# Self-attention slots of a decoder layer: output projection moved ahead of the transposes, attention times V moved behind the scores

## The reference

```
x = x + self_attention(layernorm(x))        # fixed point, 16 heads of 64
x = x + cross_attention(layernorm(x), ctx)  # 16 heads of 64
x = x + experts(layernorm(x))               # two experts of width 1024, with rank-16 updates

def make_fxp(t):   # 12 fraction bits, clipped to +-(8 - 1/4096)
    return trunc(clip(t, -c, c) * 4096) / 4096
# self-attention:
q, k, v = make_fxp(x @ Wqkv) split into heads
dots = make_fxp(q @ k.T / 8)
attn = make_fxp(softmax(dots))
out  = make_fxp(attn @ v)
out  = make_fxp(out @ Wproj + bias)
```

## Time and profile before

| | |
|---|---|
| median of the runs | 730.09 us |
| span of the profiled execution | 730.2 us |
| PE busy | 672.8 us, 92% |
| DVE busy | 550.0 us, 75% |
| ACT busy | 413.7 us, 57% |
| POOL busy | 272.6 us, 37% |
| mean granted TensorE clock | 0.995 of full |

### The profile page before, as it was taken

One profiled execution on the slowest core, in us unless ns is written; L12 is line 12 of the kernel. 1 busy time (PEld: TensorE's weight loads), 2 busy tenths in 40 slices (PEclk: granted clock), 3 DMA queues, 4 the chain that ended last, 5 costly groups with the idle time before them and its releaser, 6 DMA issues.

```text
span 730.2 us, 15676 instructions
## 1 busy us (share of the span) xinstructions
PE 672.8 (92%) x5186; PEld 551.7 (76%) x5186; DVE 550.0 (75%) x1142; ACT 413.7 (57%) x1443; POOL 272.6 (37%) x610
## 2 busy tenths in 40 slices
PE   5998879989998899878989999999999889999997
PEld 4777768777886788766777877787788777888986
DVE  5879887887888789757767776677667668787775
ACT  4677756767776777764455455445544563433432
POOL 1166754454445534535354344234333532010110
PEclk9999999999999999999999999999999999999999
DMA  9135100000000000050000000000000000000000
GB/s 312 49 111 150 60 30 1 1 1 1 0 0 0 0 0 0 0 153 1 1 2 16 1 1 1 14 0 0 0 0 0 0 1 1 2 30 0 29 29 29
DMA packets 17002, 18.75 MB, mean 26 GB/s; under 512 B 2851, under 2 KB 15427, under 8 KB 16963
## 3 DMA queue, kind: packets, MB, share of 16 engines
q1 hardware_dynamic: 15330, 15.11, 6.4%
q0 software_dynamic: 1632, 3.15, 1.5%
HBM read 16.16 MB, written 2.10 MB: 25 GB/s over the span
## 4 chain that ended last, share of the span: by engine, by line
PE 35%; POOL 7%; DVE 6%; ACT 3%; issue 3%; DVEq 0%; POOLq 0%; ACTq 0%
PE bank L405 9%; PE bank L407 8%; PE bank L406 8%; POOL p_f L363 6%; PE bank L583 3%; ACT e_sb L889 2%; PE bank L595 2%; PE bank L607 1%; DVE mx L1164 1%; PE bank L729 1%; PE bank L741 1%; DVE bn_st L966 1%; DVE oT_lo L1206 1%; POOL p_int L316 0%; DVE v_sb L1137 0%
## 5 line engine op out<-in xcount | busy, mean ns | idle before, releaser
L363 POOL TENSOR_SCALAR p_f<-e_sb,rsum 128x128 f32<-128x128 f32 x256 | 95.6, 398 | 156.7 <-DVE rsum L1199 156.7
L316 POOL TENSOR_SCALAR p_int<-e_sb,rsc 128x128 int16<-128x128 f32 x256 | 116.2, 475 | 6.3 <-issue 5.7
L889 ACT ACTIVATE e_sb<-bank,neg_max 128x128 f32<-128x128 f32 x256 | 90.1, 380 | 12.1 <-DVE neg_max L1168 11.9
L804 ACT ACTIVATE sgn<-bank 128x512 bf16<-128x512 f32 x96 | 57.2, 598 | 57.6 <-PE bank L407 57.6
L819 ACT ACTIVATE e_sb<-si 128x128 f32<-128x128 int16 x256 | 75.1, 303 | 0.0
L1021 DVE SCALAR_TENSOR_TENSOR ri<-sgn,bank 128x512 int16<-128x512 bf16 x96 | 62.5, 677 | 7.3 <-ACT sgn L804 6.5
L875 ACT COPY q_sb<-bank 128x512 f32<-128x512 f32 x32 | 18.8, 587 | 84.5 <-PE bank L407 84.5
L311 POOL TENSOR_TENSOR rsc<-rsum,growth 128x8 f32<-128x8 f32 x32 | 6.7, 209 | 156.0 <-DVE rsum L1047 156.0
L889 ACT ACTIVATION_READ_ACCUMULATOR e_sb<-bank,neg_max 128x1 f32 x256 | 55.9, 218 | 0.0
L405 PE MATMUL bank<-xnT_hi,wqkvT_lo 128*128 128x512 f32 x128 | 53.6, 419 | 2.2 <-DVE ri L1021 1.3
L1175 DVE COPY aT_sb<-bank 128x512 f32<-128x512 f32 x64 | 41.2, 685 | 12.7 <-PE bank L583 12.5
(11 more groups left out here) (162 smaller groups left out, 2039.5 us busy)
## 6 DMA issues: line engine op xcount, KB each, us to landing
x_sb<-in_x SPq DMA_DIRECT2D x4, 512.0 KB, 10.3
wqkv_raw<-in_L_attn_w_qkv SPq DMA_DIRECT2D x2, 1024.0 KB, 10.2
out<-x_sb SPq DMA_DIRECT2D x8, 256.0 KB, 2.2
wqkv_raw<-in_L_attn_w_qkv SPq DMA_DIRECT2D x2, 512.0 KB, 5.1
wp_raw<-in_L_attn_w_proj SPq DMA_DIRECT2D x1, 1024.0 KB, 12.3
raw_b<-in_L_xattn_Wq SPq DMA_DIRECT2D x2, 512.0 KB, 3.3
wq_hi<-in_L_xattn_Wq POOLq DMA_DIRECT2D x2, 512.0 KB, 4.1
wo_hi<-in_L_xattn_Wo POOLq DMA_DIRECT2D x2, 512.0 KB, 8.4
```

Of the source, the lines that this page charges most:

```text
L316: i = nc.gpsimd.tensor_scalar(p_int[:, t, :], e_sb[:, t, :], rsc[:, t:t + 1], -0.5, ALU.mult, ALU.add)
L363: i = nc.gpsimd.tensor_scalar(p_f[:, t, :], e_sb[:, t, :], rsum[:, t:t + 1], 0.0, ALU.mult, ALU.add)
L804: nc.scalar.activation(sgn[:, m % 2, :], proj_ps[m % 2][:, :], ACT.Sign).then_inc(a_sgn, 1)
L889: last = nc.scalar.activation(e_sb[:, t, :], s_ps[hh][:, (t % 4) * P:(t % 4 + 1) * P], ACT.Exp, bias=neg_max[:, t:t + 1], scale=DH ** -0.5 ...
```

## The change

On PE, project_out(n-3) moves ahead of a_transpose(n-2), and a_attend(n-2) moves from ahead of the V blocks to the slot's end, behind a_scores. On ACT, a_out_sign(n-2), which reads a_attend's result, moves behind the signs of the scores. On DVE, a_out(n-2) moves from right behind the reciprocal to the slot's end, behind the clips. No operation, size or semaphore is added or removed.

```diff
@@ -512,23 +512,23 @@
                 if first:
                     wait(pe, w_lo, (10, 0, 12, len(PREP), 0, 0, 0, 0)[s])
                 lag2 = not (first and s < 2)
+                if not (first and s < 3):
+                    project_out(n - 3, (s - 3) % NP, a_olo, a_pj, (wpT_hi, wpT_lo), (a_z, 2 * g))
                 if lag2:
                     a_transpose(n - 2)
-                if not (first and s < 3):
-                    project_out(n - 3, (s - 3) % NP, a_olo, a_pj, (wpT_hi, wpT_lo), (a_z, 2 * g))
                 if s == NP - 1:
 
                     normed_T(g + 1, lambda: wait(pe, a_ri, BLOCKS * (g + 1)))
-                if lag2:
-                    p = (s - 2) % NP
-                    gg = g if s >= 2 else g - 1
-
-                    a_attend(n - 2, p, BLOCKS * gg + (block_index(1) + 4 if p < 4 else block_index(3) + 4))
                 if s < 4:
                     for i in range(2):
                         j = 2 * s + i
                         a_block(g, base + 2 + i, (j % 4, 2 * E + 512 * (j // 4)), False)
                 a_scores(n, s, BLOCKS * g + base + 2)
+                if lag2:
+                    p = (s - 2) % NP
+                    gg = g if s >= 2 else g - 1
+
+                    a_attend(n - 2, p, BLOCKS * gg + (block_index(1) + 4 if p < 4 else block_index(3) + 4))
 
             normed_T(0, lambda: wait(pe, w_lo, 4))
             a_weights_T(PREP_PARTS[1])
@@ -840,8 +840,6 @@
                     if s == NP - 1:
                         xnT_high(g + 1)
                     a_exp(n - 1, 1)
-                if lag2:
-                    a_out_sign(n - 2)
                 if s < 4:
                     sign_of(g, base + 2)
                     sign_of(g, base + 3)
@@ -849,6 +847,8 @@
                     wait(act, a_S, 2 * n + i + 1)
                     wait(act, a_si, 2 * n + i - 1)
                     nc.scalar.activation(s_sgn[:, i, :], s_ps[i][:, :], ACT.Sign).then_inc(a_ssgn, 1)
+                if lag2:
+                    a_out_sign(n - 2)
 
             xnT_high(0)
             a_weights_high(PREP_PARTS[1])
@@ -1100,8 +1100,6 @@
                     xnT_low(g + 1)
                 if not (first and s == 0):
                     a_recip(n - 1)
-                if not (first and s < 2):
-                    a_out(n - 2)
                 if s < 4:
                     if s == 0 and not first:
                         wait(dve, a_av, NP * g - 4)
@@ -1118,6 +1116,8 @@
                 for i in range(2):
                     wait(dve, a_si, 2 * n + i + 1)
                     V.tensor_scalar(si[:, i, :], si[:, i, :], LOW, None, ALU.max).then_inc(a_clip, 1)
+                if not (first and s < 2):
+                    a_out(n - 2)
 
             xnT_low(0)
             a_weights_low(PREP_PARTS[1])
```

## The result

The changed kernel takes 783.8 us (median of 4 runs, 781.7 to 785.8) against 730.05 us: a ratio of 1.0735, interval 1.0715 to 1.0755, slower. The forecast was 782 us, 770 to 798. The profiled execution took 783.5 us and spans 781.7 from its first instruction to its last; the same 1.8 us lie between time and span in every run whose span is on record.

The account below looks back on a forecast made before the run. The prediction took an 8.35 us loop through aT, exponentials and p_int to bound short slots and PE's own work long ones; 730.2 + 45.4 (chain) + 6.5 (clock) = 782 us, range 770 to 798.

Parts of the forecast that it names:

- The loop of 8.35 us: Self-attention: transposes, aT copy, exponentials, reciprocal, p_int and next transposes form a loop that sets the slot time before the change.
- short slots: Slots 4 to 6 of a group of eight, without V blocks; predicted to go from 8.35 to 9.8 us, +1.45.
- The rival in which the projection fills the gap: The projection runs in PE's idle time if oT_lo comes by T+6.6 in short slots: 730 us, at best 707; chance 0.04.
- The rival with short slots alone: Only short slots stall, since V fixes run during the exponentials and long slots stay at 10.05: about 752 us; chance 0.08.
- The terms of the chain: Added slot times in self-attention because late a_out delays the projection and the transposes behind it: together +45.4 us.
- Long slots: Slots 0 to 3, which carry V blocks; predicted to go from 10.05 to 11.7 us, +1.65.
- With y_out: In slot 2 of a later group, y_out's two DVE operations stand in front of si too: +2.85 us.
- POOL's wo_lo beside V's fixes at the start of group 1: POOL's wo_lo stretches DVE's V fixes, 2.32 instead of 0.78 us; this 1.5 us now lies on the chain.
- The clock: Long PE gaps in self-attention lower TensorE's clock: falls at half of 15 gaps, 0.9 us each, +6.5, bounds 0 and 22.
- the rival of a fall at nearly every gap: The clock falls at nearly every gap, or in long slots too: about 797 us; chance 0.15.
- Group 0: First group of self-attention, measured from slot 2: predicted 63.65 us against 55.31, +8.3.
- POOL in the way of a_out in group 0: POOL's low parts block a_out, oT_hi meeting each of five 2.4 us operations: 794 us; chance 0.05.

Follow-up runs that it names:

- The swap of two calls on PE: The changed kernel with a_transpose(n-2) put back ahead of project_out(n-3), late a_out and late attend kept: 736.5 us, 1.0096 against the kernel before.
- y_out early: The changed kernel with transposes ahead of projection, exponentials ahead of the aT copy, y_out ahead of the reciprocal: 734.2 us, 1.0061 against the kernel before.
- the best kernel: The y_out early kernel with aT's copy between the exponentials' halves in groups 1 to 3, group 0 in the old order: 727.9 us, 0.9967.

## Why the prediction was right

*The loop of 8.35 us binds short slots; PE's idle 1.2 us is its slack.* Right. Filling the gap gave nothing (projection alone: 8.35 still), and taking aT out of the loop's way gave 8.0 and 7.6.

*The projection waits for a_out and holds the transposes.* Right: 30 waits, 56.1 us. The swap of two calls on PE gives 47 us back. The rival in which the projection fills the gap failed where it was said to: oT_lo came at T+8.1, not T+6.6. The rival with short slots alone failed as well, PE waits 1.4 to 1.5 us in long ones.

*The terms of the chain.* Short slots 9.70 for 9.8. Long slots 11.45 for 11.7: DVE's run of eight was 3.48 by starts where I had 3.57 by ends, a_out 1.86 (212.37 to 214.23) for 1.98, and the projection 1.54 for 1.60. The two blocks of PE take 3.03 us (225.44 to 228.47 in the earlier trace rows), not the 2.8 that I wrote, so PE's wait in short slots is 2.35 and not 2.6; that changes no slot, since PE waits either way. With y_out 12.65 for 12.9, slot 7 10.7 for 10.75 (both in the kernel with the K block twice, where no fall disturbs them). POOL's wo_lo beside V's fixes at the start of group 1 was on the chain as foreseen, but stretched them by 0.6 us only, not 1.5 (1.1 in the kernel with the K block twice). In the changed kernel, DVE:

```profile
107.64 1.37 DVE L1025 TENSOR_SCALAR v_sb<-ri 128x512 f32<-128x512 int16 x2
```

The span without falls, as the kernel with the K block twice has it, is 771.5 us: 730.2 + 41.3, where I had 45.4.

*The clock.* The term that was mis-sized the other way: 781.7 - 771.5 = 10.2 us, I had 6.5, well inside its bounds of 0 and 22. I had 15 long gaps, half of them with a fall at 0.9 us. There were 12 of 1.87 to 2.63 us in groups 1 to 3 and ten were followed by a fall, about 1 us each. So by number the rival of a fall at nearly every gap was the nearer one, and what held the sum down was the price. For that price the prediction's own bound was worked out too low: 2.03 us scaled by 1.98/1.09 are 1.66 us more and not 1.5, 25 us for 15 gaps and not 22. The transposes at 1.2 GHz, which no row of before showed (changed kernel, PE):

```profile
262.76 1.08 PE L464 MATMUL bank<-ident_b,p_int 128*128 128x128 bf16 x8
```

The full transposes took 1.08 us for 0.62, the projection before them 2.34 (260.42 to 262.76) for 1.54. The two errors, 4.1 too many in the chain and 3.7 too few in the clock, all but cancel, which is luck; the total is better than its parts. The base was off a little as well: a span of 730.2 belongs to an execution of an estimated 732 us, by the 1.8 us between time and span, so 782 was a forecast of the span, 781.7, rather than of the median, 783.8.

*Group 0.* 63.1 us for 63.65. No fall there, although three gaps of 2.6 were counted: its 2.4 us of idle time came in two pieces, since the scores waited 1.05 to 1.19 us for K while POOL's low parts held up the Q fix, and only 1.2 to 1.4 us were left before the projection. I had named that collision for oT_hi and not for Q; it cost no time, slots stayed at 9.70.

*POOL in the way of a_out in group 0* did not come in the changed kernel: no oT_hi or oT_lo there took over 0.75 us. It came where the order moved a_out against POOL (2.73 us for oT_lo with the transposes first, 2.49 for oT_hi with y_out early). The Trainium skill (SBUF — State Buffer, "Who interferes with whom") says that DVE in a two-port mode and GpSimd exclude each other for a whole instruction. The 2.49 us fit this, since oT_hi ends just behind wq_lo; in which mode it ran no row tells.

What stays open: the best kernel loses 1.2 us at the hand-over to cross-attention, 22.7 us from the transposes of the last slot 7 to the second ones after it, against 21.5 before. Whether another order there would keep them was not tried.

## What to carry to other kernels

An idle gap in front of a wait may be the slack of a loop through other engines: follow that loop once around, and compare its length with each engine's own work, before moving work into the gap. In an in-order queue whatever stands ahead of the head of such a loop lends it all its own waits, so a producer moved late and its consumer moved early can cost together what neither costs alone (by the ratios +54 us here, +7 and +19 apart, and the 19 are a wait for aT that the whole change does not have). Before an order is changed, look at what the moved instructions will run beside: here DVE's 0.5 to 0.7 us operations took over 2 us beside POOL's. When stalls lie between matmuls, count their effect on the clock too, and time a kernel with harmless work in the gap to see its price.

## What was not expected of the hardware

Doing the K block twice made the kernel 9.7 us faster, with the granted clock at 2.4 GHz where it had dropped to 1.2. The gaps of 1.4 to 1.5 us in the long slots of groups 2 and 3 brought no fall; of the twelve of 1.87 to 2.63 us ten did, and two, of 2.39 and 2.35 us at 159.8 and 169.5, did not, though 2.37 us at 179.2 did. Nor did 2.86 us at 112.7 in the kernel with the K block twice:

```profile
112.71 0.39 PE L405 MATMUL bank<-wpT_hi,oT_lo 128*128 128x256 f32 x1 [2.86 <-DVE oT_lo L1042]
```

So the length of a gap alone does not tell.
